# An LSTM recurrence on one core: output gates of both halves in single columns under one tanh, and a state that is split into its two parts by a scan

## The reference

```
x_proj = x @ W_ih.T + b_ih + b_hh            # 6250 x 1024
def step(carry, xp):                         # 6250 times, one after the other
    h, c = carry                             # 256 numbers each
    i, f, g, o = split(xp + h @ W_hh.T, 4)
    c = sigmoid(f) * c + sigmoid(i) * tanh(g)
    h = sigmoid(o) * tanh(c)
    return (h, c), h
logits = lstm_out @ W_lin.T + b_lin
g = argmax(logits)                           # 0 or 1
inc = cumsum(g * lstm_out)                   # then 2*lstm_out + prefix*fw + suffix*bw
```

## Time and profile before

| | us |
|---|---|
| median of 3 runs | 15350.32 |
| lowest, highest | 15345.05, 15354.82 |
| the profiled execution, its own time | 15353.04 |
| its span in the trace | 15350.2 |
| mean granted TensorE clock of it | 0.545 of full |

### The profile page before, as it was taken

How to read it: one execution, slowest core, us unless ns; L and a number is a source line. 1 busy time by engine, 2 the same in 40 slices (tenths; PEclk the granted TensorE clock), 3 DMA queues, 4 the chain that set the end, 5 groups by cost and what they waited for, 6 DMA issues and landing times. The chain is left out here.

```text
span 15350.2 us, 691245 instructions
## 1 busy us (share of the span) xinstructions
PE 9953.5 (65%) x255269; PEld 9025.8 (59%) x255269; DVE 10365.1 (68%) x84126; ACT 4955.5 (32%) x32393; POOL 2065.8 (13%) x1598
## 2 busy tenths in 40 slices
PE   3444444866666666666666666666666666666666
PEld 2333333766666666666666666666666666666665
DVE  4443222577777777777777777777777777777777
ACT  1111111333333333333333333333333333333333
POOL 5887887000000000000000000000000000000000
PEclk7666777755555555555555555555555555555556
DMA  6555555100000000000000000000000000000000
GB/s 159 89 91 85 83 83 85 59 1 1 1 1 1 1 1 1 1 1 1 1 1 1 1 1 1 1 1 1 1 1 1 1 1 1 1 1 1 1 1 17
DMA packets 617504, 301.47 MB, mean 20 GB/s; under 512 B 454943, under 2 KB 573747, under 8 KB 616843
## 3 DMA queue, kind: packets, MB, share of 16 engines
q0 software_dynamic: 150048, 204.90, 8.3%
q1 hardware_dynamic: 456678, 91.09, 3.3%
q10 hardware_dynamic: 10742, 5.06, 0.1%
HBM read 153.07 MB, written 141.27 MB: 19 GB/s over the span
## 5 line engine op out<-in xcount | busy, mean ns | idle before, releaser
L1416 PE MATMUL bank<-hp,whh 128*128 128x1 f16 (+1 forms) x200000 | 7030.9, 168 | 3793.6 <-DVE hp L1547 3793.6
L1416 PEld LDWEIGHTS bank<-hp,whh 128*128 128x128 f16 x200000 | 6519.5, 106 | 4336.8 <-DVE hp L1547 4336.0
L1481 ACT ACTIVATE gates<-bank 128x4 f32<-128x4 f32 x12500 | 2183.1, 175 | 7435.9 <-DVE bank L1519 7045.8
L1519 DVE TENSOR_REDUCE bank<-bank 128x4 f32<-128x8 f32 x12500 | 2171.4, 174 | 2666.9 <-PE bank L1416 2260.9
L1547 DVE TENSOR_TENSOR hp<-bank,sg 128x1 f16<-128x1 f32 x12500 | 2004.3, 162 | 409.3
L1490 ACT ACTIVATE bank<-gates 128x1 f32<-128x1 f32 x12500 | 2067.5, 165 | 324.3
L1552 DVE SCALAR_TENSOR_TENSOR hp<-bank,sg,hp 128x1 f16<-128x1 f32 x12500 | 2164.2, 216 | 0.0
L1416 PE MATMUL bank<-xsteps,wih 128*128 128x10 f16 (+1 forms) x40032 | 2163.9, 170 | 0.0
L1527 DVE CUSTOM_DVE_ANT_1 uv<-gates 128x4 f32<-128x4 f32 x12500 | 1994.8, 160 | 2.2
L1416 PEld LDWEIGHTS bank<-xsteps,wih 128*128 128x128 f16 x40032 | 1750.5, 104 | 0.0
L1626 POOL TENSOR_TENSOR U<-U (+1 forms) x25 | 27.6, 1140 | 12541.0 <-POOLq L1569 12541.0
(11 more groups left out here) (179 smaller groups left out, 3499.1 us busy)
## 6 DMA issues: line engine op xcount, KB each, us to landing
xsteps<-x_d SPq DMA_DIRECT2D x1252, 5.0 KB, 1.7
U<-hp SPq DMA_DIRECT2D x1250, 5.0 KB, 1.7
acc_d<-zero SPq DMA_DIRECT2D x30, 640.0 KB, 12.6
ht<-acc_d SPq DMA_DIRECT2D x75, 224.0 KB
rows<-xn_d,staged_i POOLq DMA_INDIRECT x782, 2.8
acc_d<-sums,target POOLq DMA_INDIRECT x782, 3.8
xi<-xn_d SPq DMA_DIRECT2D x50, 125.0 KB
xi<-in_x SPq DMA_DIRECT2D x50, 125.0 KB
```

The costliest lines, as they stand in the source:

```text
L1416: return nc.tensor.matmul(to, w, v, start=start, stop=True, skip_group_check=True)
L1481: nc.scalar.activation(gates[:, k, 0:2 * NG_[k]:2], zi[k], ACT.Tanh, scale=down)\
L1519: nc.vector.tensor_reduce(zi[k], gi[k][b][:, s], axis=AX.X, op=ALU.add).then_inc(ifg_summed[k], 1)
```

## The change

- `whh`'s low part is stored 2^13 times larger (`RAISE`), since the state that it meets is now unscaled (between -2 and 2, not times 2^13).
- The first state part is `hu` = (tanh of the output gate + 1) times the tanh of the cell, unscaled, in f16, in one instruction. The low weight parts are multiplied with it.
- The rest and both scaled parts follow in `parts_of_state`: a scan of two elements, with the opened gate as its initial value. Its first element is opened x `tc` - `hu`, the rest, its second that times RAISE (the column beside `tc` in PSUM holds RAISE and the one beside `hu` zero). A product by RAISE then makes the scaled value. `hp` has four f16 per state: unused, rest unscaled, rest scaled, value scaled. The pair that is stored is the last two.
- Both output gates go to `go`, a column for each half, and every product of theirs (low weight with `hu`, high weight with rest, high weight with value) is a matmul of one column into the same PSUM column. So no DVE sum is needed: one tanh on ACT reads both from PSUM. Their projection too has a matmul for each of the three products.
- Group 0 now has three gates like group 1. The low weight parts of group 1 for state half 1 come before the wait for h2_ready[0].

The core of the diff:

```diff
+HU = 0
+RAISE = float(1 << H_EXP - 1)
...
-                nc.vector.scalar_tensor_tensor(out=parts[1], in0=wT[:, u % 2, :], scalar=w_scale[:, w:w + 1], in1=parts[0],
-                                               op0=ALU.mult, op1=ALU.subtract).then_inc(w_split, 1)
+                rest = wT[:, u % 2, :] if w == 0 else parts[1]
+                last = nc.vector.scalar_tensor_tensor(out=rest, in0=wT[:, u % 2, :], scalar=w_scale[:, w:w + 1],
+                                                      in1=parts[0], op0=ALU.mult, op1=ALU.subtract)
+                if w == 0:
+                    chained(last)
+                    last = nc.vector.tensor_scalar(parts[1], rest, RAISE, None, ALU.mult)
+                last.then_inc(w_split, 1)
...
-            hp = sb("hp", [128, 2 * B, KD, PARTS], F16, st)
+            hp = sb("hp", [128, 2 * B, KD, 4], F16, st)
+            h_pairs = hp[:].rearrange("p t k c -> p (t k c)").bitcast(F32).rearrange("p (t k c) -> p t k c", k=KD, c=2)
+            hu = sb("hu", [128, 2 * B, KD, 4], F16, st)
+            opened = sb("opened", [128, KD], F32, st)
+            tc_raise = [bank[6 + k][:, 4:6] for k in range(KD)]
+            go = [bank[4 + b][:, 0:B * KD].rearrange("p (t m) -> p t m", t=B) for b in range(2)]
...
-                        sp.dma_start(Hs[:, bass.ds((2 * i + b) * B, B), :], h_pairs[:, b * B:(b + 1) * B]).then_inc(h_out[b], 16)
+                        sp.dma_start(Hs[:, bass.ds((2 * i + b) * B, B), :], h_pairs[:, b * B:(b + 1) * B, :, 1]).then_inc(h_out[b], 16)
...
+                        if g == 3:
+                            yield go[b][:, :, m], gbias[:, cols], ones[:], m == 0
+                            for p, q in ((0, 0), (0, 1), (1, 0)):
+                                for k in range(KD):
+                                    yield go[b][:, :, m], wih[:, p, k, cols], xs_[:, b, q, k, :], False
...
-                per_step = GC * (1 + PARTS * KD) // B
+                per_step = -(-(3 * KD * (1 + PARTS * KD) + KD * (1 + 3 * KD)) // B)
...
+                    def output_gates():
+                        for m in range(KD):
+                            cols = slice((KD * 3 + m) * 128, (KD * 3 + m + 1) * 128)
+                            for k in range(KD):
+                                matmul(go[b][:, s, m:m + 1], whh[:, 1, k, cols], hu[:, before, k, HU:HU + 1], False)
+                                for q in (3, 2):
+                                    last = matmul(go[b][:, s, m:m + 1], whh[:, 0, k, cols],
+                                                  hp[:, before, k, q:q + 1], False)
+                        return last
...
                     pe.wait_ge(h1_ready[0], t + 1)
+                    rest_of_weights(0, 0)
+                    rest_of_weights(1, 0)
                     pe.wait_ge(h1_ready[1], t + 1)
+                    rest_of_weights(0, 1)
+                    rest_of_weights(1, 1)
                     pe.wait_ge(h2_ready[0], t + 1)
+                    weights(0, 0)
                     pe.wait_ge(h2_ready[1], t + 1)
+                    weights(0, 1).then_inc(ifg_made[0], 1)
+                    weights(1, 0)
+                    weights(1, 1).then_inc(ifg_made[1], 1)
+                    output_gates().then_inc(o_made_, 1)
...
                     def tanh_o():
-                        act.wait_ge(o_summed, t + 1)
-                        nc.scalar.activation(og[1], zo[:], ACT.Tanh, scale=down).then_inc(o_act, 1)
+                        act.wait_ge(o_made_, t + 1)
+                        nc.scalar.activation(gates[:, :, 6], go[b][:, s], ACT.Tanh, scale=down).then_inc(o_act, 1)
...
+                    def open_states():
+                        dve.wait_ge(o_act, t + 1)
+                        nc.vector.tensor_scalar(opened[:], gates[:, :, 6], 1.0, None, ALU.add).then_inc(opened_ready, 1)
+
+                    def state(k):
                         dve.wait_ge(tc_ready[k], t + 1)
                         if s == 0 and due(16 * i):
                             dve.wait_ge(h_out[b], 16 * i)
-                        nc.vector.tensor_tensor(hp[:, at, k, 0:1], tc[k], sg[:, k:k + 1], ALU.mult)\
-                          .then_inc(h1_ready[k], 1)
-
-                    def state2(k):
+                        stt(out=hu[:, at, k, HU:HU + 1], in0=gates[:, k, 6:7], scalar=1.0, in1=tc[k], op0=ALU.add,
+                            op1=ALU.mult).then_inc(h1_ready[k], 1)
+
+                    def parts_of_state(k):
                         dve.wait_ge(h1_ready[k], t + 2)
-                        stt(out=hp[:, at, k, 1:2], in0=tc[k], scalar=sg[:, k:k + 1], in1=hp[:, at, k, 0:1],
-                            op0=ALU.mult, op1=ALU.subtract).then_inc(h2_ready[k], 1)
+                        if not k:
+                            dve.wait_ge(opened_ready, t + 1)
+                        nc.vector.tensor_tensor_scan(hp[:, at, k, 1:3], tc_raise[k], hu[:, at, k, 0:2],
+                                                     opened[:, k:k + 1], ALU.mult, ALU.subtract)
+                        nc.vector.tensor_scalar(hp[:, at, k, 3:4], hu[:, at, k, HU:HU + 1], RAISE, None, ALU.mult)\
+                          .then_inc(h2_ready[k], 1)
 
                     sum_gates(0)
                     sum_gates(1)
-                    sum_o()
                     new_cell(0)
-                    open_state(0)
                     new_cell(1)
-                    open_state(1)
-                    state1(0)
-                    state1(1)
-                    state2(0)
-                    state2(1)
+                    state(0)
+                    open_states()
+                    state(1)
+                    parts_of_state(0)
+                    parts_of_state(1)
```

More of the change, by code:

```diff
@@ L1432, in body, with rest_of_weights @@
                     before = (b * B + s - 1) % (2 * B)
-                    def gates_of(m, k, p):
-                        for g in range(NG_[m]):
+                    def rest_of_weights(m, k):
+                        for g in range(3):
                             cols = slice((KD * g + m) * 128, (KD * g + m + 1) * 128)
-                            last = matmul(gi[m][b][:, s, g, 0:PARTS - p], whh[:, p, k, cols],
-                                          hp[:, before, k, 0:PARTS - p], False)
-                        return last
@@ L1441, in ogate, with weights @@
-                    def ogate(k, p):
-                        cols = slice((KD * 3 + 1) * 128, (KD * 3 + 2) * 128)
-                        return matmul(go[b][:, s, 0:PARTS - p], whh[:, p, k, cols],
-                                      hp[:, before, k, 0:PARTS - p], False)
+                            matmul(gi[m][b][:, s, g, 0:1], whh[:, 1, k, cols], hu[:, before, k, HU:HU + 1], False)
+                    def weights(m, k):
+                        for g in range(3):
+                            cols = slice((KD * g + m) * 128, (KD * g + m + 1) * 128)
+                            last = matmul(gi[m][b][:, s, g, :], whh[:, 0, k, cols], hp[:, before, k, 2:4], False)
+                        return last
@@ L1480, in tanh_gates @@
                         act.wait_ge(ifg_summed[k], t + 1)
-                        nc.scalar.activation(gates[:, k, 0:2 * NG_[k]:2], zi[k], ACT.Tanh, scale=down)\
+                        nc.scalar.activation(gates[:, k, 0:6:2], zi[k], ACT.Tanh, scale=down)\
                           .then_inc(ifg_act[k], 1)
                     def tanh_o():
-                        act.wait_ge(o_summed, t + 1)
-                        nc.scalar.activation(og[1], zo[:], ACT.Tanh, scale=down).then_inc(o_act, 1)
+                        act.wait_ge(o_made_, t + 1)
+                        nc.scalar.activation(gates[:, :, 6], go[b][:, s], ACT.Tanh, scale=down).then_inc(o_act, 1)
                     def tanh_cell(k):
@@ L1507, in _ @@
                 nc.vector.memset(gates[:, :, 5:6], 0.0)
+                for k in range(KD):
+                    nc.vector.memset(tc_raise[k][:, 1:2], RAISE)
+                nc.vector.memset(hu[:], 0.0)
                 nc.vector.memset(hp[:], 0.0).then_inc(lstm0, 1)
```

57 lines of the change are left out of this document (14 added, 43 removed).

## The result

| | before | after |
|---|---|---|
| median, us | 15351.3 (15345.1 to 15354.8) | 15580.9 (15576.0 to 15581.7) |
| ratio, 95% | | 1.0149 (1.0132 to 1.0167) |
| profiled execution, us (span) | 15353.0 (15350.2) | 15580.6 (15578.8) |
| mean step of the recurrence, us | 1.950 | 1.987 |

The account below looks back on a forecast made before the run. Bound taken as a ring of short instruction latencies, 1.950 us a step, no engine full. Per step 0.212 - 0.070 - 0.107 = +0.035, about 225 us, plus some 2 for raised weights: 15577 us; range 15115 to 15950.

Parts of the forecast that it names:

- TensorE gives back 0.107: Matmuls between the step's last wait and the second reduce: 9 instead of 13, 0.107 us a step earlier.
- One wait instead of two at the state, 0.070: DVE's state product after the cell tanh: one wait lets it start 0.03 behind instead of 0.10, minus 0.07 us.
- The tail, plus 0.212: DVE from state(1) to the end of product(1): 0.667 us instead of 0.455, so plus 0.212 a step.
- Both waits are satisfied by then.: At scan(0), behind state(1): neither of its two waits still waits; the hand-over was taken as 0.183 us.
- `opened`, "price nothing, cover 0.03": DVE's `opened` between the two states: clear at 1.23, state(1)'s input at 1.26, so no cost, 0.03 us cover.
- this ring is the one to price: The chain of half k = 1, from second reduce to second reduce: 1.95 us, the whole step.
- In one step of five it has a second, long satisfied, which lies under the wait.: At the new `state`: a second wait in one step of five, already satisfied, adding nothing to the step.
- the likeliest case: Whole kernel: slower by 1.5%, own range 15480 to 15720 us, chance 58%.
- The output gates' tanh: On ACT, 0.76 us after the last wait, ahead of half 0's cell tanh with some 0.04 to spare.
- The store: Store of five steps in 1280 pieces of 4 bytes: lands in an estimated 4.7 us, price nothing.
- Faster by a cheaper hand-over: From state(1) to scan(0): event and ALU_OP cost 0.11 us, minus 0.073 a step, 15120 us; faster case 25%.
- a register rebuilt each time: At the wait of `opened_ready`: an extra ALU_OP costs some 0.09 us a step, 16140 us; slower-by-more case 10%.

## Why the prediction was right

The mechanism was right in its large terms. By its own steps:

- **TensorE gives back 0.107.** Confirmed: from the weight load behind the last wait to the second reduce 0.442 pass instead of 0.55. Three of the four matmuls were undone and cost 0.080. That the same move would give less in the kernel before was seen only afterwards: such a gain holds only if TensorE has room ahead of the wait.
- **One wait instead of two at the state, 0.070.** Confirmed by 0.825 against 0.895 after the reduce, and shown by itself by the swap of two lines in the kernel before, where state(1) moved from 0.895 to 0.825 too.
- **The tail, plus 0.212.** Measured 1.471 - 0.825 = 0.646 against the 0.455 of before: plus 0.191. Hand-over 0.176 (0.183), scan to product 0.138 and 0.128 (0.132), product to scan 0.059 (0.068), product 0.145 (0.152). The scan took 0.218 (0.216). The Trainium skill (DVE: opcode table, § 6 Datapath and trigger behaviour) says that the scan runs at half throughput; the prediction's estimate was 0.211 by that rule and 0.47 at full throughput, and the trace, with 0.218, agrees with the rule, if the fixed part of the 250-element row holds for these operands. By itself a scan of two elements can't tell: the plain instruction of one takes as long.
- **"Both waits are satisfied by then."** This is the sentence that failed. One was not: `opened` ends at 0.897 and the event instruction that waits for it stands at 0.935, 0.110 after state(1) has started. The two instructions by themselves take 0.166, and `opened` sets the rest.
- **`opened`, "price nothing, cover 0.03".** It starts at 0.734, behind state(0), and state(1) is not delayed. But the cover was measured against the wrong instruction: who waits for `opened` is the scan, and it costs some 0.010. Half 0 then sets the step, not half 1 ("this ring is the one to price"), though by so little that the sum along half 1 came out nearly right. The kernel with the high parts early shows it: half 1 earlier by 0.08, the step unchanged.
- **"In one step of five it has a second, long satisfied, which lies under the wait."** Failed for one step in ten: the register of line 1558 is made by an ALU_OP, which takes the wait for the cell tanh, and state(0) follows at 0.756 instead of 0.662. In the kernel before the same instruction made state(0) of step 0 just as late (0.760 instead of 0.668), but state(1), behind its event instruction, came at 0.896 in any case. Now the delay passes through `opened` to the scan one for one: plus 0.093 in step 0. It doesn't hang on `opened` alone: with `opened` early, where that is not late, step 0 is still 0.093 longer, since state(1) starts at 0.894 instead of 0.826 and the scan at 1.014 instead of 0.923. Step 1 is 0.006 longer than the regular ones; no run ties that to step 0, and with the code shifted step 1 is regular and step 3 has it.
- **Nothing was said of step 6**, plus 0.100, and what makes it stays open.

The regular step is the sum again with measured terms: 0.191 - 0.070 - 0.107 = +0.014, and the step grew by 0.016, from a mean of 1.9504 to 1.9667 (the forecast had 0.035). In us of the kernel: 6250 x 0.0163 = 102, steps 0 and 1 of each ten 625 x 0.099 = 62, step 6 625 x 0.100 = 62, the later start 2.7, together 229; the profiled executions differ by 227.5. The regular step was forecast at 6250 x 0.035 = 219 (the prediction writes 221 and then 225, a few us more than its terms give: 4 x 0.027 is 0.108, and with 0.034 it would be 212). So 117 us too much there met 124 us that were not priced at all. The total is right to 4 us by that coincidence; without the two long steps it would have been some 15457, outside the own range of the likeliest case (15480 to 15720), though still on its side.

- **The output gates' tanh** is out of the way as forecast: it starts at 9001.58, 0.76 behind the last wait's first weight load, and the cell tanh of half 0 at 9001.72, when its input is there. **The store** landed after 2.5 us (the estimate was 4.7) and nothing waits for it. The Trainium skill (DMA: Bandwidth & Descriptors, § Rules for kernel authors) warns of one descriptor per element: the packets of the whole kernel rise from 617504 to 2057505, which is 1250 times the 1152 more pieces of a store, so the trace agrees; the run with that alone shows no time for it. **The clock** stayed.
- **The rivals.** *Faster by a cheaper hand-over* named the right place, but did not occur: an event and an ALU_OP together cost 0.166, not 0.11. Only without the event instruction is it 0.098, and then the kernel is 2.2% faster (15014; the rival had 15120 for its own reason). *No change*, *a register rebuilt each time*, *the store stalls* and *the clock rises* did not occur; line 1563 runs 6240 times, once a step.

## What to carry to other kernels

- Where an instruction has several waits, write the one that comes last first (an ALU_OP that makes a register for a wait takes that place, as step 0 shows). The swap of two lines gave 480 us here, where the whole rearrangement of the arithmetic cost 230.
- Price a wait by what it waits for, not by the engine that runs it: "long satisfied" has to be shown with the end of the producer beside the start of the sequencer's instruction. Look at every position of an unrolled body, since a counter that is made in one of ten steps can take a wait with it.
- A total that comes out right is no proof of its terms. Two unpriced stalls of 62 us each hid that the regular step was 0.018 us shorter than forecast, and that another half set it.

## What the runs showed of the hardware

- An instruction whose own wait comes last follows ACT's end by 0.03 us. Through an event instruction it is 0.10 to 0.11. The instruction behind an event starts 0.066 after the event (state products and scans), 0.076 for the plain rest, 0.099 for the cell update with the store's wait moved.
- Between two short DVE instructions without data to wait for, an ALU_OP makes the second start 0.098 to 0.109 after the first, and an ALU_OP and an event 0.166 (0.18 between the two of the earlier trace rows).
- A scan of two elements from PSUM with a pointer as scalar: 218 ns in the mean, within 1 ns of the plain one-element instruction with those operands.
- With DVE's instructions at one place in memory one step of ten lost 0.100 us between an event and the scan; with 24 instructions more ahead of the loop it did not. The cause is open.
- 1280 pieces of 4 bytes instead of 128 of 40 landed in 2.5 instead of 1.7 us, 1250 times, at no cost in time.
